# One barrier between stages, an earlier set-up, broadcast scan corrections and another order of the last mixes in a two-layer recurrent kernel

## What is computed

```python
xn = layernorm(x)
s = recurrence(xn, ...)        # layer 1: gated linear recurrence, 4 heads
g = silu(moe(xn, ...))         # router softmax, 257 best tokens of each sequence and expert, gelu
x = x + s * g
xn = layernorm(x)
s = scan(xn, steps_raw, G_raw, A_raw, B_mat, C_mat, D_vec)
g = silu(ffn(xn, w1, w3, w2))  # 8 experts by position, silu(gate) * up
x = x + s * g

# scan: z, y are the two states of each of 64 channels, u is B_mat applied to xn
S = 1 + steps * G;  alpha = 1.99 * tanh(steps**2 * A / S / 1.99)
z[t] = z[t-1] / S - alpha / steps * y[t-1] + F1[t]
y[t] = steps / S * z[t-1] + (1 - alpha) * y[t-1] + F2[t]
out  = y applied to C_mat + xn * D_vec
```

## Time and profile before

| what | us |
|---|---|
| median of 3 runs | 4386.11 |
| the runs | 4384.94 to 4389.0 |
| the profiled execution, its time | 4401.49 |
| its span, first to last instruction | 4399.7 |
| PE busy | 4125.3 (94%) |
| DVE busy | 2703.7 (61%) |
| ACT busy | 1936.3 (44%) |
| POOL busy | 1696.7 (39%) |

### The profile page before, as it was taken

One profiled execution on the slowest core, in us unless ns is written; L12 is line 12 of the kernel. 1 busy time (PEld: TensorE's weight loads), 2 busy tenths in 40 slices (PEclk: granted clock), 3 DMA queues, 4 the chain that ended last, 5 costly groups with the idle time before them and its releaser, 6 DMA issues. The chain is left out here.

```text
span 4399.7 us, 72682 instructions
## 1 busy us (share of the span) xinstructions
PE 4125.3 (94%) x28636; PEld 3270.7 (74%) x28636; DVE 2703.7 (61%) x5040; ACT 1936.3 (44%) x3576; POOL 1696.7 (39%) x1337
## 2 busy tenths in 40 slices
PE   8699999999999998899999999999995999999995
PEld 8656656656656655798898988888895888888884
DVE  7467777777777776344434343444432688888885
ACT  2134444444444444445444444545442444444441
POOL 2234334334334332444434444444433234444443
PEclk9999999999999998999999999999997999999998
DMA  9501011011011010333323232332224344454433
GB/s 313 168 25 35 30 39 35 30 40 35 30 40 35 30 40 20 92 49 59 62 42 65 47 61 43 66 51 57 43 40 98 98 102 110 100 116 112 106 68 43
DMA packets 254003, 294.21 MB, mean 67 GB/s; under 512 B 21600, under 2 KB 226656, under 8 KB 251616
## 3 DMA queue, kind: packets, MB, share of 16 engines
q0 software_dynamic: 88064, 117.74, 15.8%
q1 hardware_dynamic: 165600, 171.82, 12.1%
HBM read 155.15 MB, written 134.35 MB: 66 GB/s over the span
## 5 line engine op out<-in xcount | busy, mean ns | idle before, releaser
L564 DVE TENSOR_TENSOR e_hTl<-e_hf,e_hTh 128x512 fp32r<-128x512 f32 x512 | 354.6, 692 | 800.5 <-ACT e_hTh L506 752.2
L1077 POOL TENSOR_TENSOR a_mix<-a_tmp,a_h 128x512 f32<-128x512 f32 x320 | 389.9, 1238 | 793.8 <-PE ps L1376 745.1
L425 POOL DMA_INDIRECT acc_d<-e_y,e_sids x256 | 409.0, 1598 | 707.4 <-DVE e_y L580 654.6
L505 ACT ACTIVATE e_hf<-ps_heads,e_b 128x512 f32<-128x512 f32 x512 | 355.4, 694 | 677.3 <-PE ps_heads L663 620.8
L663 PE MATMUL ps<-e_w2h,e_hTh 128*128 128x256 f32 x2048 | 578.8, 283 | 0.0
L663 PE MATMUL ps<-e_w2h,e_hTl 128*128 128x256 f32 x2048 | 577.3, 282 | 0.0
L663 PE MATMUL ps<-e_w2l,e_hTh 128*128 128x256 f32 x2048 | 571.3, 279 | 1.0 <-issue 1.0
L663 PE MATMUL ps_heads<-e_xTh,e_w1h 128*128 128x512 f32 x1024 | 418.4, 409 | 16.2 <-ACT e_hTh L506 8.8
L663 PE MATMUL ps_heads<-e_xTh,e_w1l 128*128 128x512 f32 x1024 | 405.5, 396 | 0.0
L663 PE MATMUL ps_heads<-e_xTl,e_w1h 128*128 128x512 f32 x1024 | 405.4, 396 | 0.0
L663 PEld LDWEIGHTS ps<-e_w2h,e_hTh 128*128 128x128 f32 x2048 | 385.7, 188 | 20.4
(11 more groups left out here) (293 smaller groups left out, 9218.0 us busy)
## 6 DMA issues: line engine op xcount, KB each, us to landing
r_x<-in_L_attn_hidden_states SPq DMA_DIRECT2D x32, 512.0 KB, 6.2
xn_d<-r_xn SPq DMA_DIRECT2D x32, 512.0 KB, 4.8
xnT_d<-r_xT SPq DMA_DIRECT2D x32, 512.0 KB, 3.8
acc_d<-a_zeros POOLq DMA_DIRECT2D x32, 512.0 KB, 3.0
s_d<-a_s SPq DMA_DIRECT2D x32, 512.0 KB, 2.8
e_w<-in_L_ffn_w SPq DMA_DIRECT2D x16, 1024.0 KB
f_a<-acc_d SPq DMA_DIRECT2D x32, 512.0 KB, 3.8
f_x<-s_d SPq DMA_DIRECT2D x32, 512.0 KB, 5.2
```

The lines of the kernel that those rows point to most:

```text
L425: pool.indirect_dma_start(acc_d, bass.IndirectOffsetOnAxis(ap=sids[:, GT * q + t:GT * q + t + 1], axis=0), ys[r][:, t, :], None, compute_o ...
L505: nc.scalar.activation(hf[m % 2][:], ps[2 + m % 2][:], ACT.Gelu, bias=b1s[:, m:m + 1])
L564: nc.vector.tensor_tensor(hT[q % 2][1][:, m, :], hf[m % 2][:], hT[q % 2][0][:, m, :].bitcast(F32), ALU.subtract).then_inc(h_sb, 1)
L1077: nc.gpsimd.tensor_tensor(mix[n][:, m, :].rearrange("p (c t) -> p c t", c=GT), tmp[i % 2][:].rearrange("p (c t) -> p c t", c=GT), h[q % 2] ...
```

## The change

One barrier stands where two with the clearing between them stood; the semaphores of the first two stages are cleared at the start of the experts, those of the last two at the end. The block for `ident` is gone, and its two instructions open routing. The tables of the recurrence and of the scan, and their semaphores, are made ahead of routing (`recurrence_tables`, `scan_tables`), and the set-up that used them moves into routing: loads on SP, clearing in pieces after each power on POOL, coefficients, masks, powers, the centred weight and the first `a_lerp` on DVE, sigmoid and tanh on ACT.

In routing's SP list, `begin_in` and three loads of the scan's tables and `tables_in` (the 22 loads of the recurrence) come in the last group, ahead of the store of the turned groups 30 and 31, and six loads of 256 bytes stand ahead of the first group:

```diff
+            def begin_in():
+                hT_v = xnT_d.rearrange("k p (b t) -> k p b t", t=T)
+                for r in range(RING):
+                    sp.wait_ge(xT_out[r], 16 * (NG // RING // 2))
+                for q in range(2):
+                    for k in range(KD):
+                        sp.dma_start(h[q][:, k, :, 1:P + 1], hT_v[k, :, GT * q:GT * (q + 1), 0:P]).then_inc(h_in[q], 16)
...
+                if last and r == RING - 1:
+                    begin_in()
+                    sp.dma_start(bm[:], w["L1_attn_B_mat"]).then_inc(raw_in, 16)
+                    sp.dma_start(cm[:], w["L1_attn_C_mat"]).then_inc(raw_in, 16)
+                    sp.dma_start(dv[:], w["L1_attn_D_vec"].to_broadcast([P, D])).then_inc(raw_in, 16)
+                    tables_in()
                 if not first or r:
                     store_turned(g - 1, (r - 1) % RING)
...
             for r in range(1, RING):
                 load(r, r)
+            for c in range(2):
+                for n, name in enumerate(("L1_attn_steps_raw", "L1_attn_G_raw", "L1_attn_A_raw")):
+                    sp.dma_start(raw[c * PS:(c + 1) * PS, n:n + 1], w[name]).then_inc(raw_in, 16)
```

In POOL's list, `prepare` clears some tiles after each power (at most 1024 columns at a time, the masks' `row` and `col` in group 17), and two subtractions follow the last group:

```diff
                     nc.gpsimd.tensor_tensor(rstd[r][:], vare[r][:], r_power[:], ALU.pow).then_inc(rstd_ready, 1)
+                    prepare(2 * i + r)
+            for r in range(2):
+                pool.wait_ge(h_in[r], 32)
+                nc.gpsimd.tensor_tensor(delta[r][:], h[r][:, :, :, 0:P], h[r][:, :, :, 1:P + 1], ALU.subtract
+                                        ).then_inc(deltas, 1)
```

```diff
             statistics(0, 0)
+            dve.wait_ge(raw_in, 16 * 6)
...
             each_group(dve, one)
+
+            dve.wait_ge(alpha_out, 1)
...
+            dve.wait_ge(w_in, 16 * (LOADS + 1))
...
             dve.wait_ge(logit_sb, NG)
...
+            dve.wait_ge(deltas, 1)
...
             dve.wait_ge(score_t, 1)
```

ACT's list:

```diff
+            act.wait_ge(raw_in, 16 * 6)
+            nc.scalar.activation(raw[:, 0:1], raw[:, 0:1], ACT.Sigmoid).then_inc(sig, 1)
             each_group(act, one)
+            act.wait_ge(alpha_in, 1)
+            nc.scalar.activation(raw[:, 3:4], raw[:, 3:4], ACT.Tanh, scale=1.0 / 1.99).then_inc(alpha_out, 1)
+            act.wait_ge(raw_in, 16 * 9)
+            nc.scalar.copy(bmp[0][:], bm[:]).then_inc(bm_high, 1)
             logits(NG - 1, RING - 1)
```

```diff
-        SPREAD = {QB - 1: (2, 2, 2, 2, 1, 1), 0: (2, 2, 2, 2, 1, 1), 1: (2, 2, 2, 2, 1, 1), 2: (2, 2, 2, 2, 1, 1)}
+        SPREAD = {QB - 1: (2, 2, 2, 2, 1, 1), 0: (2, 2, 1, 1, 1, 1), 1: (2, 1, 1, 1, 1, 1), 2: (1, 1, 1, 1, 1, 1)}
+                    q, adds = divmod(s - FIX, 2)
+                    rows, shape = slice(GT * q, GT * (q + 1)), [P, GT, NSB, SBLK]
+                    o.n = FIX_N + 2 * (s - FIX)
                     o.wait()
+                    if not adds:
+                        for n, v in enumerate((zc, yc)):
+                            o.did(nc.vector.tensor_tensor(
+                                fix[n][:], v[r][:, rows, 0:NSB].unsqueeze(3).to_broadcast(shape),
+                                qy[:, 1:SBLK + 1, n].unsqueeze(1).unsqueeze(1).to_broadcast(shape), ALU.mult))
+                    else:
+                        own = ends[:, rows]
+                        o.link(nc.vector.tensor_tensor(own, own, fix[0][:], ALU.add))
+                        o.did(nc.vector.tensor_tensor(own, own, fix[1][:], ALU.add))
+            def gated_last(q):
+                g = TILES - QB + q
+                gated(g, g % PAIR, 2 * (q % 2))
+                if q:
+                    dve.wait_ge(c_sb, g + 1)
+                    dve.wait_ge(gs_sb, 2 * g + 2)
+                    nc.vector.tensor_tensor(xd[g % PAIR][:], xd[g % PAIR][:], gs[g % PAIR][:], ALU.mult
+                                            ).then_inc(o_last, 1)
             each_tile(dve, tile)
-            for s in range(sum(SPREAD[QB - 1]), STEPS):
-                scan(NE - 1, 1, s)
-            for g in range(TILES - LAG, TILES):
-                gated(g, g % PAIR)
+            s = sum(SPREAD[QB - 1])
+            for g in range(TILES - LAG, TILES - QB):
+                gated(g, g % PAIR)
+                scan(NE - 1, 1, s)
+                scan(NE - 1, 1, s + 1)
+                s += 2
+            for s in range(s, FIX):
+                scan(NE - 1, 1, s)
+            for q in range(QB):
+                scan(NE - 1, 1, FIX + 2 * q)
+                scan(NE - 1, 1, FIX + 2 * q + 1)
+                if q:
+                    gated_last(q - 1)
+            gated_last(QB - 1)
...
+            def mix_last(q):
+                pe.wait_ge(scan_o, SCANS * (NE - 1) + FIX_N + 4 * (q + 1))
```

More of the change, by code:

```diff
@@ L43 @@
 REST = FF - (FC - 1) * P
+PADDED = 7
+SET = PADDED + 13
+READY = SET + NH + 2
+LOADS = 21
+COEFS = 12
 class Order:
@@ L90, in sb @@
             return mem.enter_context(nc.sbuf_tensor(name, shape, dt))
-        sem = phase_semaphores(nc, mem)
+        mem.callback(nc.all_engine_barrier)
+        (mu, w1, w2, b2, b2t, xo, xot, xb, rw, kw, vw, gw, dw1, dw2, db, bonus, gnw, gnb, ow, power, h, delta,
+         lerp, low, x1t, dlow, heads, A2, S, Sd, vmean, mask, col, row, bits, shifted, after, one_level, rowb,
+         rowf, zeros, w_in, set_up, masks, h_in, deltas, lerped, vw_centred, zeroed) = tables
+        (bm, bmp, cm, dv, raw, coef, qz, qt, qy, raw_in, coef_o, power_o, sig, alpha_in, alpha_out, bm_high,
+         bm_split, begun) = scan_t
+        m11, m12, near, drive_scale, far = (coef[:, n:n + 1] for n in range(5))
         RING = 4
@@ new lines, in _ @@
+            dve.wait_ge(alpha_out, 1)
+            o.link(nc.vector.tensor_scalar(m12, al, -1.99, None, ALU.mult))
+            o.link(nc.vector.tensor_scalar(near, m12, 1.0, None, ALU.add))
+            o.link(nc.vector.tensor_tensor(near, near, m11, ALU.add))
+            assert o.n == COEFS
+            o = Order(dve, masks, 2)
+            dve.wait_ge(masks, 2)
+            o.link(nc.vector.tensor_tensor(bits[:], row[:], col[:], ALU.bitwise_xor))
+            o.link(nc.vector.tensor_tensor(after[:], col[:], row[:], ALU.is_gt))
@@ new lines, in _ @@
+            for lv in range(LEVELS - 2):
+                o.link(nc.vector.tensor_scalar(shifted[:], bits[:], lv, None, ALU.logical_shift_right))
+                o.link(nc.vector.tensor_scalar(one_level[:], shifted[:], 1.0, None, ALU.is_equal))
+                o.link(nc.vector.tensor_tensor(mask[lv][:], one_level[:], after[:], ALU.mult))
+            o.link(nc.vector.tensor_scalar(rowb[:], row[:, 0:1], B - 1, None, ALU.bitwise_and))
+            o.link(nc.vector.tensor_scalar(rowf[:], rowb[:], float(T), None, ALU.mult))
@@ new lines, in _ @@
+            dve.wait_ge(begun, 4)
+            o = Order(dve, power_o)
+            dve.wait_ge(coef_o, COEFS)
+            for n in range(SBLK):
+                o.link(nc.vector.tensor_scalar(qt[:], qy[:, n, :], m12, None, ALU.mult))
+                o.link(stt(out=qz[:], in0=qz[:], scalar=m11, in1=qt[:], op0=ALU.mult, op1=ALU.add))
+                o.link(nc.vector.tensor_tensor(qy[:, n + 1, :], qz[:], qy[:, n, :], ALU.add))
+            dve.wait_ge(bm_high, 1)
+            nc.vector.tensor_tensor(bmp[1][:], bm[:], bmp[0][:].bitcast(F32), ALU.subtract).then_inc(bm_split, 1)
```

493 lines of the change are left out of this document (253 added, 240 removed).

## The result

The changed kernel takes 4348.72 us (median of 5, 4344.87 to 4351.53) beside 4386.11 for the kernel before: ratio 0.9912, 95% interval 0.9901 to 0.9924, so 37.4 us faster. A repetition on another chip gave 4343.69 beside 4382.08, ratio 0.9912 (0.9899 to 0.9926). The forecast was 4347.

What follows compares the result with a forecast made beforehand. PE is busy 94% of the span, so only stage boundaries and the end can be won. Terms -4.8 - 3 - 0.5 - 10.7 - 6 - 14.5 = -39.5 from 4401.5 give 4362, less 15.4: 4347; range 4335 to 4359, with rivals 4325 to 4371.

Steps and rivals of the forecast that it cites:

- Start of routing: Routing's start: DVE waits for six small loads and ten links, so PE starts at 15.8 instead of 11.74, +4.1.
- The set-up inside routing: End of routing: moved DVE work follows ACT's tanh, softmax at 194.5, PE's first recurrence product 208.3 instead of 213.15, -4.8.
- ACT's table load: Before routing's softmax: ACT's change of function may load its table after its wait, +1.3 (0 to 1.3).
- The delta's wait: Recurrence's start: the second subtraction is done before, so DVE's 3.4 us of waiting go, -3 (0 to -3.4).
- The barriers: Between stages: one barrier for two and a clearing saves half of 1.4 us, -0.7 each.
- Layer two's set-up: Experts to layer two: earlier first load, shared first product, powers moved away, PE's 3.99 us wait gone, -10.7 (-8 to -13).
- Corrections: Layer two's steady experts: 16 instructions of 128 x 512 for 32 cut DVE's work and PE's waits, -6 (-12 to 0).
- The end: After layer two's last tile: corrections in groups between mixes, POOL's last issue at 4375.4 instead of 4389.90, -14.5 (-10 to -18).
- The shift to the median: Whole kernel: the profiled execution lay 15.4 above the median of 4386.1, so the same is taken off.
- The set-up is hidden after all: Routing: the tanh comes early enough for DVE's 19.3 us to fit its slack, softmax 16 us earlier, 4331; 10%.
- The broadcast is dear: Layer two's corrections: 8 multiplications at 1.2 add 4 us of DVE work an expert, +24 in all, 4371; 13%.
- The other two: Slower than before: all 16 correction instructions at 1.2 and more, 4%. Nothing changes: new waits take all the gains, 3%.

Runs made afterwards that it cites:

- run 1: Changed kernel with ACT's tanh ahead of its 32 groups instead of behind them; 4338.05 us beside 4386.6, ratio 0.9891.
- run 3: Changed kernel with DVE's ten coefficient links behind its ninth group instead of between the first two statistics; 4341.86 us, ratio 0.9901.
- run 5: Run 4 with PE waiting for the centred weight only before the first product that reads it; 4321.48 us beside 4382.08, ratio 0.9865.
- run 9: Changed kernel with layer two's old end (whole scan first, seven mixes, all products on POOL), broadcast corrections kept; 4376.91 us beside 4403.0, ratio 0.9942.
- run 2: Run 1 with the centred weight also back in the recurrence, behind DVE's first eight largest; 4338.71 us, ratio 0.9892.
- run 11: Changed kernel with two barriers instead of one behind each of the four stages; 4374.57 us beside 4403.0.
- run 8: Changed kernel with DVE's 48 links of powers back in layer two, behind its first turned tile; 4341.21 us, ratio 0.9909.
- run 10: Run 9 with the old corrections too (32 instructions of 128 x 128, old spread over the tiles); 4372.81 us, ratio 0.9933.
- run 7: Changed kernel with corrections for one block of eight (128 x 64 instead of 128 x 512); 4323.81 us, ratio 0.9867.
- run 12: Run 5 with no correction steps in the last two parts of tiles 1 and 2; 4360.74 us beside 4404.88, ratio 0.9904.
- run 4: Changed kernel with coefficients behind DVE's ninth group, tanh behind ACT's fifteenth, centred weight back in the recurrence; 4337.83 us, ratio 0.9891.

## Why the prediction was right, and which steps were not

The sum came out, 4347 for 4348.7, but not all of its terms did. The set-up and the order at the end are shown by runs 1, 3, 5 and 9; the step on the corrections failed. That the median lies within 2 us of the forecast is in part luck: by the traces the change gave 4.9 less than forecast, and single stretches of the same code vary by as much.

**Start of routing**: right, +4.5 for +4.1. Run 3 takes it away. The sum has a slip: eleven issues of 0.6 from 0.73 on end at 7.3, as measured (7.31), not at 6.3; DVE went on behind the last of the six loads at 10.89, not 10.2.

**The set-up inside routing**: right in mechanism and size. "DVE's 24.3 us of slack are spent waiting" shows as 20.22 us, and the softmax came at 194.59 for 194.5. Run 1 shows it: only the place of one ACT instruction changes, and 10.7 us go. (The 29.2 us of waiting that the prediction counts from the end of the softmax count from PE's last product in it, at 183.97.) Missing from the step was what would be late next: the tables' landing at 182.4, and with it gone PE's own wait for `a_vw` (runs 1, 2 and 5).

**ACT's table load** (+1.3): wrong, 0. I put it behind ACT's wait. It ran at 178.71, before the wait for DVE; the softmax was over at 205.64 for 206.9, and PE started 1.3 earlier than forecast, 207.04 for 208.3. (0.7 and 0.5 behind 206.9 make 208.1; measured from the softmax's end to PE's product are 1.40.) The Trainium skill (ScalarE: Activation LUTs, "Step-by-step: what each stage is for") says that the load stands right before the ACTIVATE; the trace agrees with the order, and adds that here the wait belongs to the ACTIVATE, 17.1 us later, not to the load. The row that I took as a model, the silu's load, stands behind a wait for a transfer in the changed kernel too (3348.35). The silu waits for two semaphores and the exp for one; whether that decides the order, no run varied.

**The delta's wait** (-3): PE's next long wait ended 5.96 earlier, at 240.97, just as far as PE's start had moved. Two things lie in that sum. PE's products on `a_low` and `a_x` behind them took 2.4 us more, seen at the first `a_dw` (220.32 against 223.99, 3.7 earlier and not 6.1); and the earlier interpolation gave 2.3 back. The first belongs to the execution: the same kernel again has 2.10 for the products on `a_low`, and ends that wait at 239.37, 7.6 earlier than before with a start only 5.4 earlier. To POOL's first instruction of the experts the gain is 8.0, against 4.8 + 3 + 0.5 = 8.3. That this agrees so well is luck: the recurrence's stretch takes 1544.1 to 1549.8 in traces of the same code.

**The barriers** (-0.7 each): mis-sized. Run 11 puts a second one at 0.15 to 0.3. Between experts and layer two 5.8 went, of which 5.4 are the nine loads; 0.5 is left for a barrier and the clearing.

**Layer two's set-up** (-10.7): right. -5.8, -1.5 and the 4.0 us of waiting make -11.3. Run 8 brings the wait back, 4.7.

**Corrections** (-6): the step that failed is "PE's waits that this can reach are 1.7 an expert ... Net -0.9 x 7". DVE's share was well sized: 97.3 us busy an expert before and 95.2 after, -2.1 for -2.3. What did not hold is that PE's waits follow it. Between the traces before and after they seem to: in the window of the waits shown above, the kernel before has

```profile
PE ps L2155 <- DVE f_hTh L1842: 8.1, 12, 1.0
PE ps_heads L2122 <- DVE f_xTl L1842: 6.6, 16, 2.6
PE ps L2122 <- DVE f_hTl L1842: 4.0, 1, 4.0
```

that is 14.7 besides the first `f_hTl`, against 12.9. But run 10 has the old form and 11.8, and ten traces with the new form and spread have 12.4 to 13.6; from first to last tile runs 9 and 10 take the same. So the old form's two traces lie on both sides of the new form's, and no saving of 6 us shows. Only the place of the waits changed: in five steady experts PE waits 4.7 us for `f_hTh` and 0.5 for `f_hTl` with the new form, and 4.0 for `f_hTh` and 2.3 for `f_xTl` with the old one in run 10. My reading is that half as many steps, nearly twice as long, stand in front of the low parts that PE wants; run 7, with additions of 0.22 for 0.69 in the same places, shows that the steps cost PE at all, run 12 that their places matter; that the length of a step cancels the saving is not shown. The stretch still gained 3.5 besides the 4 us of waiting, and that is within what the same kernel varies by: 892.9 and 896.9.

**The end** (-14.5): right in mechanism, mis-sized by 2.7. The first correction came 9.3 later in relation to the last tile (forecast 8.7), and the rest took 24.8 for 22.7: two stops by POOL instead of one, and a second wait for PE, whose last mixes take 3.78 at half clock. Order 9.9 and form 1.8 (runs 9 and 10) make the 11.7.

**The shift to the median** (-15.4): right. By the traces it lay in the experts' stretch (16.3), which the change does not touch.

**Rivals.** *The set-up is hidden after all* did not happen, but runs 1 to 5 show what it is worth: the forecast's 16 us on top of the start's 5.6, measured 22.2. *The broadcast is dear*: it takes 0.69 alone at the end. In the steady stretch it takes 0.89 and 1.52 on average, by POOL's products and not by the broadcast, and DVE's busy time fell. The other two did not come.

## What to carry to other kernels

Work moved into an engine's idle time must be reachable before that time starts: look at the engine that releases it and at what that engine's list waits for ahead of it. When a wait is taken away, look for the next one by its place in the list and not by where the data is used. An engine that saves 2 us of work need not give its reader anything (runs 9 and 10); look at the piece in front of the reader's own operand. Where the pieces stand can cost more (18 us in run 12) than what a cheaper form saves.

## What the runs showed of the hardware

**POOL stops a DVE instruction for about as long as POOL's own still has to run.** In run 7 two additions of 128 x 64, which take 0.22, fell under POOL's product at the end (timelines of DVE and POOL):

```profile
4304.50 0.22 DVE L2033 TENSOR_TENSOR f_fix<-f_yc,f_qy 128x64 f32<-128x64 f32 x1
4304.75 1.18 DVE L2038 TENSOR_TENSOR f_U<-f_U,f_fix 128x64 f32<-128x64 f32 x1
4305.97 1.19 DVE L2039 TENSOR_TENSOR f_U<-f_U,f_fix 128x64 f32<-128x64 f32 x1
...
4304.54 2.53 POOL L1905 TENSOR_TENSOR f_xd<-f_xd,f_g 128x512 f32<-128x512 f32 x2 [11.45 <-DVE f_xd L2052]
```

Each lost about 0.96 us, one to each half of POOL's 2.53, of which about 1.1 were left when it started; the stopped instructions of 128 x 512 in the changed kernel lost 1.07 and 0.94 (1.76 and 1.63 for 0.69). POOL pays as well: its two halves at 4322.19 took 3.30 us, where they took 2.53 beside the small additions. The Trainium skill (SBUF — State Buffer, "SBUF: two separate sides") calls it an exclusive lock and not a split of bandwidth; the trace agrees, since with a split the loss would have grown with the size of the instruction.

**The same code varies with the granted clock.** Windows of two experts of the changed kernel (length, busy of PE, PEld, DVE, ACT, POOL, then the granted clock):

```profile
3591.57:3708.53 116.96, 111.79 (x626) 97.31 (x625) 95.28 (x186) 54.68 (x92) 49.46 (x36) 0.99 0.48 110
3708.53:3826.67 118.14, 113.03 (x626) 98.20 (x625) 95.25 (x187) 54.74 (x92) 49.43 (x36) 0.97 0.48 109
```

The same instructions take 1.2 us more where 0.97 was granted on average. Layer two has five experts with work like these, and its stretch from first to last tile in eight traces of the same code lies between 892.9 and 898.9. That is as much as several of the edits are worth, and it is the part of run 4's loss that lies in layer two.

**The experts' stretch has two lengths**, 1571 to 1578 and 1590 to 1599, with the same code. In the long ones the waits of PE for ACT's `e_hTh` come to 8.8 us (before) and 9.0 (run 9), in the changed kernel's trace there is none. PE is also busy longer, 1562.5 us before against 1556.3 in the changed kernel; the two make 15.0 of the 16.3. The long ones are the trace before and those of the chips on which the kernel before takes 4403.0 and 4404.9, whatever the edit. What makes ACT late there was not tried.
